# Rows for a gather pass: GpSimd's indirect gathers, and one tile in 64 by one-row transfers from SyncE

## The chip, the cores and the metric

The program runs on one core of a Trainium2 chip. The metric is the device time of one execution in microseconds; it is given as the median of several runs. The core has five engines that run side by side: TensorE (PE), VectorE (DVE), ScalarE (ACT), GpSimd (POOL) and SyncE (SP). SP and ACT issue direct DMAs, POOL issues indirect ones (a gather of rows by a list of row numbers).

## The reference, cut to what matters

A graph with 12,500 nodes of 128 features and 200,000 edges, sorted by destination. Four layers follow each other, each a sum over the edges of rows of a table with one row per node:

```
edge_index = jnp.stack([src, dst])
h = jnp.maximum(_layernorm(x, axis=-1), 0.0)
x = x + _L0_gnn_ref(h, edge_index, W1, b1, W2, b2)     # two graph convolutions: segment_sum(h[s] * norm, d)
h = jnp.maximum(_layernorm(x, axis=-1), 0.0)
x = x + _L1_gnn_ref(h, W, b, src, dst)                 # segment_sum(features[src], dst)
h = jnp.maximum(_layernorm(x, axis=-1), 0.0)
x = x + _L2_gnn_ref(h, edge_index, edge_weight, W, b)  # weighted segment_sum(x_lin[row] * norm, col)
h = jnp.maximum(_layernorm(x, axis=-1), 0.0)
x = x + _L3_gnn_ref(h, node_vec1, src, dst, ...)       # attention: exp, silu(bn(.)), segment_sum(msg, dst)
```

So the rows `table[src[e]]` are needed for all 200,000 edges, five times over: passes 0 to 2 (parts of bf16), pass 3 (weighted, f32), pass 4 (attention).

## The kernel before, in words

The edges stand in 1,563 tiles of 128 edges, eight tiles to a group (GT), 196 groups (TGROUPS). The nodes stand in 98 windows of 128. Before each pass the node table is written to HBM: `table16` (`table_parts`) for passes 0 to 2, 768 bytes a row in three parts of bf16, `table` for pass 3, 512 bytes a row in f32.

In a pass, four engines work in step through semaphores:
- POOL (`gather_tiles`, issue on L447) gathers one tile by one indirect DMA: partition e of the tile gets the table's row of edge e, by the numbers in `idx_tab`. The tiles go to a ring of eight groups (RGROUPS, 64 tiles) in SBUF. From group 8 on it waits at `s_free` until the group that held the place before is released.
- SP (`relay_rows`) waits at L456 until all tiles of a group have landed (`gathered`, one semaphore per group of the ring, its due count from `landed_count`), and hands the group over by one count of `s_landed`, two groups (LEAD) ahead of the release. For the release of group g it waits on `s_prod` for the number that the table RELEASE gives (read by `table_values`, L471, four at a time) and counts up `s_free` (L467). In the kernel before this is written out group by group.
- TensorE multiplies each tile with a one-hot matrix of its destinations and adds into PSUM, one bank per window (L604 in passes 0 to 2, L677 in pass 3), sixteen items to a half, in loops (`halves_in_loops`); it waits for `s_landed` and for open banks. It reads where each item goes by loads of 32 words (`plan_values`, L508).
- ScalarE or VectorE builds the one-hot matrices (L554 and L561, or L642) and the other one empties the banks (L583, L658).

`pass_in_parts` runs passes 0 to 2, `pass_with_weights` pass 3. Pass 4 has its own code, with the same gathers from `ptable`.

The setup (one block of the program) loads and reorders the index tables. On SP it starts with two loads of every 128th destination (L793, L796, into `last_i`, semaphore `s_last`); copies of the edge arrays follow (L803 to L809), and the load of `src` into `idx_tab` (L811 to L816). VectorE waits for `s_last` before L937 and computes from it the tile numbers (L947) with which POOL starts its first gathers (L764). `Steps` counts the serial steps of VectorE on `s_dve`; other engines wait for fixed counts of it.

## Time and profile before

| | us |
|---|---|
| Median of 3 runs | 11,316.48 |
| Lowest and highest | 11,309.37, 11,317.57 |
| The profiled execution | 11,348.41 |
| Its span, first to last instruction | 11,346.6 |
| Granted share of TensorE's clock over the span | 0.597 |

The profile's page gives busy time per engine, groups of instructions by line, and the idle time of the engine before them with the engine that ended it. "Issue" as a releaser means that the engine waited for nothing that the profile shows. Register work, semaphore instructions and the issue of DMAs are not busy time; SP does only these, so its busy time isn't listed, and its instructions are read from the timeline and from the view of one source line. PEq, SPq and the like are the sequencers of the engines.

### The profile page before, as it was taken

To read this page: it belongs to the slowest core of one execution; us is meant where nothing else is said; L and a number is where in the kernel's file an instruction comes from. 1 tells how busy PE (TensorE), PEld (TensorE's weight loads), DVE (VectorE), ACT (ScalarE), POOL (GpSimd) and SP (SyncE) were. 2 spreads that over 40 slices of the span, in tenths; PEclk is the share of its full clock that TensorE was granted. 3 is DMA by queue.
4 is the path that set the end of the run, shared out by engine and by line. 5 is a ranking of instruction groups with operands and counts; after the bars stand their busy time and mean duration, and the time that the engine had idled before them with its cause. 6 is when DMAs were issued, how large, how long until landed. Compare 5 with 4: busy or idle time off the path is not lost. (4 is left out here: it accounts for less than half of the span.)

```text
span 11346.6 us, 83949 instructions
## 1 busy us (share of the span) xinstructions
PE 4273.1 (38%) x19462; PEld 3000.1 (26%) x19463; DVE 3429.0 (30%) x7384; ACT 3213.0 (28%) x7261; POOL 8251.9 (73%) x8365
## 2 busy tenths in 40 slices
PE   1222222342222223223333433333354333334687
PEld 0111111121111112111111333333354333333576
DVE  4000001110001112000000422222235677777898
ACT  3333333343333334333333300000021111111465
POOL 5777777757777775777777677777766777777676
PEclk5555555665555555555555665655676555555799
DMA  4222222232222223222222212221214555555454
GB/s 104 78 79 79 79 79 79 74 87 79 79 79 79 79 79 100 78 79 79 78 78 78 62 52 52 52 52 53 53 46 137 156 159 164 164 164 168 149 168 134
DMA packets 676090, 1067.87 MB, mean 94 GB/s; under 512 B 150850, under 2 KB 518729, under 8 KB 648857
## 3 DMA queue, kind: packets, MB, share of 16 engines
q0 software_dynamic: 329072, 676.05, 22.8%
q10 hardware_dynamic: 247712, 225.10, 6.1%
q1 hardware_dynamic: 98985, 163.50, 4.4%
q14 instruction: 249, 2.04, 0.1%
q8 instruction: 72, 1.18, 0.0%
HBM read 904.63 MB, written 161.05 MB: 94 GB/s over the span
## 5 line engine op out<-in xcount | busy, mean ns | idle before, releaser
L447 POOL DMA_INDIRECT big<-table_parts,tile_cols x4689 | 4453.3, 950 | 1593.1 <-issue 1428.9
L604 PE MATMUL psum<-big 128*128 x4992 | 1724.3, 504 | 4129.3 <-SPq L456 4030.3
L604 PEld LDWEIGHTS psum<-big 128*128 128x128 bf16 x4992 | 663.9, 140 | 4928.4 <-issue 2683.2
L447 POOL DMA_INDIRECT big<-ptable,tile_cols x1563 | 1512.1, 967 | 498.7 <-issue 476.3
L447 POOL DMA_INDIRECT big<-table,tile_cols x1563 | 1485.9, 951 | 478.7 <-issue 476.2
L561 ACT ACTIVATE big<-big,ones 128x2048 bf16<-128x2048 bf16 x312 | 624.4, 2001 | 3707.5 <-PE psum L604 2469.5
L554 ACT ACTIVATE big<-iota_col,dl_tab 128x128 bf16<-128x128 f32 x4992 | 1490.6, 387 | 33.7 <-PEq L731 13.3
L1617 PE MATMUL psum<-acc,big 128*128 x3328 | 788.4, 420 | 1217.5 <-DVE big L1594 1205.1
L583 DVE TENSOR_REDUCE acc<-psum 128x128 f32<-128x384 f32 (+1 forms) x196 | 109.7, 560 | 3648.4 <-PE psum L608 1829.2
L677 PE MATMUL psum<-big 128*128 x3328 | 751.9, 418 | 1201.8 <-SPq L456 750.1
L1617 PEld LDWEIGHTS psum<-acc,big 128*128 128x128 f32 x3328 | 704.9, 317 | 1300.9 <-issue 1300.6
L677 PEld LDWEIGHTS psum<-big 128*128 128x128 f32 x3328 | 702.7, 322 | 1252.4 <-issue 633.9
L642 DVE TENSOR_SCALAR big<-iota_col,dl_tab,ew_tab 128x128 f32<-128x128 f32 x1664 | 438.4, 364 | 1516.8 <-PE psum L677 1510.0
L1571 DVE TENSOR_REDUCE wide<-big 128x128 f32<-128x2048 f32 x208 | 766.2, 3684 | 3.2 <-ACT big L1650 3.2
L1594 DVE SCALAR_TENSOR_TENSOR big<-big,sc,psum 128x130 f32<-128x130 f32 x1664 | 516.7, 344 | 567.6 <-SPq L456 332.7
L583 DVE TENSOR_REDUCE big<-psum 128x128 f32<-128x384 f32 x98 | 54.7, 558 | 1766.2 <-PE psum L604 1764.9
L658 ACT COPY acc<-psum 128x128 f32<-128x128 f32 x98 | 26.1, 267 | 1899.1 <-PE psum L677 1899.1
L1835 PE MATMUL psum<-big 128*128 128x129 f32 x3328 | 545.8, 298 | 37.2 <-POOL big L1756 35.0
L1755 POOL TENSOR_TENSOR big<-big,tile_cols 128x2048 f32<-128x2048 f32 x104 | 376.2, 3617 | 111.0 <-ACT big L1796 110.8
L1835 PEld LDWEIGHTS psum<-big 128*128 128x128 f32 x3328 | 427.3, 194 | 66.3 <-issue 51.4
L1650 ACT ACTIVATE big<-big 128x2048 f32<-128x2048 f32 x104 | 199.6, 1920 | 718.2 <-DVE wide L1575 713.8
L608 PE MATMUL psum<-big 128*128 x1664 | 349.2, 210 | 0.0
(300 smaller groups left out, 4274.1 us busy)
## 6 DMA issues: line engine op xcount, KB each, us to landing
big<-dl_rows ACTq DMA_DIRECT2D x104, 1024.0 KB
zrows<-big ACTq DMA_DIRECT2D x104, 1024.0 KB
big<-zrows SPq DMA_DIRECT2D x104, 1024.0 KB
big<-table_parts,tile_cols POOLq DMA_INDIRECT x4689, 2.6
table_parts<-big SPq DMA_DIRECT2D x42, 672.0 KB, 3.5
big<-table,tile_cols POOLq DMA_INDIRECT x1563, 2.5
big<-ptable,tile_cols POOLq DMA_INDIRECT x1563, 2.6
ptable<-big SPq DMA_DIRECT2D x14, 455.0 KB, 3.9
```

Source lines behind the costliest of these rows:

```text
L447: pool.indirect_dma_start(out=slots[:, t % (groups * GT), 0:width], out_offset=None, in_=tab, in_offset=bass.IndirectOffsetOnAxis(ap=idx_t ...
L554: last = nc.scalar.activation(apart_flat[:, u * P:(u + 1) * P], iota_col[:], ACT.Abs, bias=dl_tab[:, col:col + 1], scale=-1.0)
L561: nc.scalar.activation(half, apart_flat, ACT.Relu, bias=ones[:, 0:1], scale=-1.0).then_inc(s_onehot, 1)
L604: last = nc.tensor.matmul(held, m, rows_t, start=False, stop=False, skip_group_check=True)
L608: last = nc.tensor.matmul(held, m, weights, start=False, stop=False, skip_group_check=True)
L642: last = nc.vector.tensor_scalar(wide_onehot[:, q % 2 * HALF + u, :], iota_col[:], dl_tab[:, col:col + 1], ew_tab[:, col:col + 1], ALU.is_ ...
L677: last = nc.tensor.matmul(held, wide_onehot[:, a % 2 * HALF + u, :], rows_t, start=False, stop=False, skip_group_check=True)
L1571: nc.vector.tensor_reduce(part[:, k, :], rows_of, AX.X, ALU.add).then_inc(s_part, 1)
L1594: last = nc.vector.scalar_tensor_tensor(zbuf[:, h, u, 0:ACW], dyn(ring_flat, slots[u], ACW), in_win[:, h, u:u + 1], bank[n % Z_BANKS][:, 0 ...
L1617: last = nc.tensor.matmul(bank[u % Z_BANKS][:, 0:ACW], onehot_t[:, h, u * P:(u + 1) * P], dyn(acc_flat, at[u], ACW), start=True, stop=True)
L1755: nc.gpsimd.tensor_tensor(m[:, :, 0:F], m[:, :, 0:F], over_f(weights_of(q), HALF), ALU.mult)
L1835: nc.tensor.matmul(dyn(sums_at, at[u], SCW), onehot[:, q % 2 * HALF + u, :], msg[q % MSGS][:, u, 0:SCW], start=False, stop=False, skip_gro ...
```

## The change

In passes 0 to 3 (`no < PASSES - 1`), the last tile of every eighth group (`SIDE`: groups 8, 16, ... 184, 23 of them) is no longer gathered by POOL. SP fetches its 128 rows by 128 transfers of one row each from the table in HBM, at an address that it holds in a register, into the same place of the ring. It does so in a loop over turns of eight groups (`relay_with_side_rows`): after handing over a group and releasing another it issues 21 or 22 rows, in six steps of eight (SIDE_STEPS); ahead of the seventh hand-over it waits for all of them (`s_side`) and clears the semaphore. The row numbers are loaded 32 words at a time (SIDE_LOAD) from `side_of`, two tables (4 partitions of 23 x 32 words) that the setup loads from `src` by two more DMAs and VectorE multiplies by the bytes of a row, 768 and 512. The counts of the semaphores follow: `landed_count` leaves the tile out, `s_last` is due at 64 in place of 32, and the steps of VectorE have one more. Hand-overs before and behind the loop are written out by `relay_steps`. The tensor `rows` gets more partitions, not more columns. Pass 4 keeps `relay_rows`, which now calls `relay_steps`.

```diff
@@ -10,6 +10,8 @@
 READY_STEP = 4
 RGROUPS = 8
 LEAD = 2
+SIDE_FIRST, SIDE_EVERY, SIDE_STEPS = 8, 8, 6
+SIDE_LOAD = 32
 Z_RGROUPS = 4
 Z_LEAD = 2
 BLOCK = 8
@@ -75,6 +77,11 @@
     RSLOTS = RGROUPS * GT
     assert TGROUPS == -(-NT // GT) and 2 * SLOTS * ACW >= RSLOTS * F
     NTAB = NI + BODY
+    SIDE = list(range(SIDE_FIRST, TGROUPS - RGROUPS + LEAD + 1, SIDE_EVERY))
+    SIDE_SPAN = SIDE_EVERY * GT * P
+    SIDE_BASE = (SIDE_FIRST + 1) * GT * P - SIDE_SPAN
+    SIDE_TURNS = len(SIDE)
+    assert SIDE_FIRST == SIDE_EVERY == RGROUPS and RGROUPS - SIDE_STEPS == LEAD and SIDE_BASE + len(SIDE) * SIDE_SPAN <= E
     CHUNKS = NW // CW
     assert CHUNKS * CW == NW and NI % P == 0 and TILES >= TROWS >= NT
     IG = NI // P
@@ -178,10 +185,13 @@
         w_z = sb("w_z", [P, 2, SCW])
         b1c = sb("b1c", [P, HM])
         score_tab = ew_tab[:, 0:NI]
-        rows_all = sb("rows", [13, max(7 * SCW, NI // 2, PLAN_HALVES * PLAN_WORDS)])
+        SIDE_PARTS = P // SIDE_LOAD
+        rows_all = sb("rows", [64 + SIDE_PARTS, max(7 * SCW, NI // 2, PLAN_HALVES * PLAN_WORDS)])
         rows = rows_all[0:1, 0:7 * SCW].rearrange("o (a f) -> o a f", f=SCW)
 
 
+        assert SIDE_TURNS * SIDE_LOAD <= rows_all.shape[1]
+        side_of = [rows_all[32 * k:32 * k + SIDE_PARTS, 0:SIDE_TURNS * SIDE_LOAD].bitcast(i32) for k in (1, 2)]
         WIN, SLOT = (rows_all[k:k + 1, :].bitcast(i16) for k in range(1, 3))
         READY, RELEASE = (rows_all[k:k + 1, :].bitcast(u16) for k in range(3, 5))
         SUM_AT = rows_all[5:6, :].bitcast(i16)
@@ -427,13 +437,18 @@
         gathered = [sem(f"gathered{k}") for k in range(RGROUPS)]
         s_landed = [sem(f"rows_landed{no}") for no in range(PASSES)]
         s_free = sem("rows_free")
+        s_side = sem("side_rows")
 
         def tiles_of(g):
             return min(GT, NT - g * GT)
 
+        def has_side(no, g):
+
+            return no < PASSES - 1 and g in SIDE
+
         def landed_count(no, g):
 
-            return 16 * sum(tiles_of(k) for n in range(no + 1)
+            return 16 * sum(tiles_of(k) - has_side(n, k) for n in range(no + 1)
                             for k in range(g % RGROUPS, g + 1 if n == no else TGROUPS, RGROUPS))
 
         def gather_tiles(pool, no, tab, slots, groups, width):
@@ -442,29 +457,67 @@
             for g in range(TGROUPS):
                 if g >= groups:
                     pool.wait_ge(s_free, freed + g - groups + 1)
-                for k in range(tiles_of(g)):
+                for k in range(tiles_of(g) - has_side(no, g)):
                     t = g * GT + k
                     pool.indirect_dma_start(
                         out=slots[:, t % (groups * GT), 0:width], out_offset=None, in_=tab,
                         in_offset=bass.IndirectOffsetOnAxis(ap=idx_tab[:, t // P, t % P:t % P + 1], axis=0),
                     ).then_inc(gathered[g % RGROUPS], 16)
 
-        def relay_rows(sp, no, groups, lead, s_done, done0):
-
-            def landed(g):
-                sp.wait_ge(gathered[g % RGROUPS], landed_count(no, g))
-                sp.sem_inc(s_landed[no], 1)
-
-            for g in range(lead):
-                landed(g)
-            for g in range(TGROUPS):
+        def relay_steps(sp, no, steps, groups, lead, s_done, done0):
+
+            for g in steps:
                 if g + lead < TGROUPS:
-                    landed(g + lead)
-                if g + groups < TGROUPS:
+                    sp.wait_ge(gathered[(g + lead) % RGROUPS], landed_count(no, g + lead))
+                    sp.sem_inc(s_landed[no], 1)
+                if 0 <= g < TGROUPS - groups:
                     if g % 4 == 0:
                         releases = table_values(sp, RELEASE, g, 4, NI)
                     sp.wait_ge(s_done, releases[g % 4] + done0)
                     sp.sem_inc(s_free, 1)
+
+        def relay_rows(sp, no, groups, lead, s_done, done0):
+
+            relay_steps(sp, no, range(-lead, TGROUPS), groups, lead, s_done, done0)
+
+        def relay_with_side_rows(sp, no, tab, slots, width, kind, row_bytes):
+
+            flat, size = tab.rearrange("n f -> (n f)").unsqueeze(0), row_bytes // width
+            items0 = no * NI
+
+            def landed_in_turn(turn, g):
+                counts = [landed_count(no, n * SIDE_EVERY + g) for n in range(SIDE_TURNS)]
+                assert all(c == counts[0] + n * (counts[1] - counts[0]) for n, c in enumerate(counts))
+                return turn * (counts[1] - counts[0]) + counts[0]
+
+            def fetch(turn, j, numbers):
+                for e in range(j * P // SIDE_STEPS, (j + 1) * P // SIDE_STEPS):
+                    if e % SIDE_LOAD == 0:
+                        numbers.clear()
+                        words = [nc.alloc_registers(f"side{no}_{e + i}", engines=[SP]) for i in range(SIDE_LOAD)]
+                        c = e // SIDE_LOAD
+                        nc.regs_load(words, side_of[kind][c:c + 1, bass.ds(turn * SIDE_LOAD, SIDE_LOAD)])
+                        numbers.extend(nc.snap(word, engines=[SP], donate=True, min_val=0, max_val=(N - 1) * row_bytes,
+                                               guaranteed_mod_val=0, out_of_modulus=row_bytes) for word in words)
+                    at = numbers[e % SIDE_LOAD] // size
+                    sp.dma_start(slots[e:e + 1, GT - 1, 0:width], flat[:, bass.ds(at, width)]).then_inc(s_side, 16)
+
+            relay_steps(sp, no, range(-LEAD, 0), RGROUPS, LEAD, s_prod, items0)
+            with sp.Fori(0, SIDE_TURNS) as turn:
+                numbers = []
+                for j in range(SIDE_EVERY):
+                    if j == SIDE_STEPS:
+                        sp.wait_ge(s_side, 16 * P)
+                        sp.sem_clear(s_side)
+                    sp.wait_ge(gathered[(j + LEAD) % RGROUPS], landed_in_turn(turn, j + LEAD))
+                    sp.sem_inc(s_landed[no], 1)
+                    if j % 4 == 0:
+                        releases = table_values(sp, RELEASE, turn * SIDE_EVERY + j, 4, NI)
+                    sp.wait_ge(s_prod, releases[j % 4] + items0)
+                    sp.sem_inc(s_free, 1)
+                    if j < SIDE_STEPS:
+                        fetch(turn, j, numbers)
+            relay_steps(sp, no, range(SIDE_TURNS * SIDE_EVERY, TGROUPS), RGROUPS, LEAD, s_prod, items0)
 
         def table_values(eng, tab, start, n, largest):
 
@@ -544,7 +597,7 @@
 
                 @block.sync
                 def _(sp):
-                    relay_rows(sp, no, RGROUPS, LEAD, s_prod, items0)
+                    relay_with_side_rows(sp, no, table16, ring16, NPARTS * F, 0, 2 * NPARTS * F)
 
                 @block.scalar
                 def _(act):
@@ -630,7 +683,7 @@
 
                 @block.sync
                 def _(sp):
-                    relay_rows(sp, no, RGROUPS, LEAD, s_prod, items0)
+                    relay_with_side_rows(sp, no, table, ring32, F, 1, 4 * F)
 
                 @block.vector
                 def _(dve):
@@ -796,6 +849,9 @@
                     sp.dma_start(last_i[0:LASTS - many * P, many:many + 1], rest).then_inc(s_last, 16)
                 else:
                     sp.sem_inc(s_last, 16)
+                side_src = src[SIDE_BASE:SIDE_BASE + len(SIDE) * SIDE_SPAN].rearrange("(k s) -> k s", s=SIDE_SPAN)[:, SIDE_SPAN - P:]
+                for to in side_of:
+                    sp.dma_start(to.rearrange("c (k e) -> c k e", e=SIDE_LOAD), side_src.rearrange("k (c e) -> c k e", e=SIDE_LOAD)).then_inc(s_last, 16)
                 sp.wait_ge(s_pad, 4)
                 full = (NT - 1) * P
                 for rows_of, a, pad, s_copied in ((dst_rows, dst, pads.bitcast(i32)[:, P:2 * P], s_rows),
@@ -913,7 +969,7 @@
                     if 1 <= t <= CHUNKS:
                         ln.relu(act, t - 1, (t - 1) % 2)
 
-                act.wait_ge(s_dve, 15)
+                act.wait_ge(s_dve, 16)
                 nc.scalar.activation(deg_r, deg, ACT.Sqrt).then_inc(s_cnt, 1)
                 act.wait_ge(s_srck, -(-TB // 4))
                 for t in range(CHUNKS + 1):
@@ -932,8 +988,10 @@
                 nc.vector.memset(tile_cnt[:, NW:NW + 1], float(E // P))
                 dve.wait_ge(s_const, 1)
                 nc.vector.tensor_scalar(is_node[:], node_id[:, 0:NW], float(N), None, ALU.is_lt)
-                dve.wait_ge(s_last, 32)
-                step = Steps(dve, s_dve, 0, 3)
+                dve.wait_ge(s_last, 64)
+                nc.vector.tensor_scalar(side_of[0], side_of[0], 2 * NPARTS * F, None, ALU.mult)
+                step = Steps(dve, s_dve, 0, 4)
+                step(nc.vector.tensor_scalar(side_of[1], side_of[1], 4 * F, None, ALU.mult))
                 nc.vector.tensor_scalar(last_wi, last_i, P.bit_length() - 1, None, ALU.arith_shift_right)
                 step(nc.vector.tensor_scalar(last_pi, last_i, P - 1, None, ALU.bitwise_and))
                 nc.vector.tensor_copy(last_w, last_wi)
@@ -949,7 +1007,7 @@
                 step.end()
 
                 dve.wait_ge(s_starts, 1)
-                step = Steps(dve, s_dve, 3, 10)
+                step = Steps(dve, s_dve, 4, 10)
                 step(nc.vector.tensor_tensor(bound[:, 0:NW], bank[5][:, 0:NW], wplus1[:, 0:NW], ALU.add))
 
                 step(nc.vector.tensor_tensor(le, bound[:, 0:NW].unsqueeze(1).to_broadcast([P, IG, NW]),
@@ -1034,7 +1092,7 @@
                     if 2 <= t < IG + 2:
                         keep_dl(t - 2)
 
-                step = Steps(dve, s_dve, 3 + 10, 3)
+                step = Steps(dve, s_dve, 4 + 10, 3)
                 dve.wait_ge(s_degrees, 1)
                 step(nc.vector.tensor_tensor(deg, bank[4][:, 0:NW], row_ptr[:, 0:NW], ALU.subtract))
                 nc.vector.tensor_scalar(no_edges[:], deg, 0.0, None, ALU.is_equal)
@@ -1061,7 +1119,7 @@
                     nc.tensor.matmul(bank[4][:, 0:NW], below[:, b, :], same[:, b, :], start=b == 0, stop=False)
                     last = nc.tensor.matmul(bank[4][:, 0:NW], ones[:], before[:, b, :], start=False, stop=b == IG - 1)
                 last.then_inc(s_counted, 1)
-                pe.wait_ge(s_dve, 3)
+                pe.wait_ge(s_dve, 4)
                 nc.tensor.matmul(bank[5][:, 0:NW], first, tile_cnt[:, 1:NW + 1], start=True, stop=True).then_inc(s_starts, 1)
                 pe.wait_ge(s_weights, 16 * 17)
                 nc.tensor.transpose(bank[6][:, 0:F], wload[:, 0, :], ident[:])
```

## Rows read from the trace of the kernel before

**Rows 1.** The page: busy times, the gathers' groups, a landing time.
```profile
PE 4273.1 (38%) x19462; PEld 3000.1 (26%) x19463; DVE 3429.0 (30%) x7384; ACT 3213.0 (28%) x7261; POOL 8251.9 (73%) x8365
...
L447 POOL DMA_INDIRECT big<-table_parts,tile_cols x4689 | 4453.3, 950 | 1593.1 <-issue 1428.9
L447 POOL DMA_INDIRECT big<-ptable,tile_cols x1563 | 1512.1, 967 | 498.7 <-issue 476.3
L447 POOL DMA_INDIRECT big<-table,tile_cols x1563 | 1485.9, 951 | 478.7 <-issue 476.2
...
big<-table_parts,tile_cols POOLq DMA_INDIRECT x4689, 2.6
```

**Rows 2.** Busy time by stretch: passes 0, 3 and 4 (last: DMA share, GB/s).
```profile
core 0: us, PE busy (x) PEld busy (x) DVE busy (x) ACT busy (x) POOL busy (x), PEclk, DMA share, GB/s
268.00:2227.00 1959.00, 567.92 (x1668) 217.25 (x1667) 126.74 (x388) 703.94 (x1765) 1482.81 (x1563) 0.55 0.29 79
...
6459.00:8420.00 1961.00, 759.58 (x3317) 702.40 (x3316) 437.54 (x1662) 51.47 (x194) 1484.79 (x1562) 0.59 0.20 52
8570.00:10558.00 1988.00, 782.78 (x3304) 699.76 (x3304) 1419.97 (x2679) 230.30 (x306) 1511.71 (x1563) 0.57 0.55 161
```

**Rows 3.** Waits of POOL, passes 0 to 3: us in total, times, longest.
```profile
POOL big L447 <- issue: 1905.2, 6248, 0.3
```

**Rows 4.** Waits of SP in pass 0: us in total, times, longest.
```profile
SPq L456 <- DMA big<-table_parts,tile_cols: 1902.0, 196, 12.1
```

**Rows 5.** Timeline of TensorE in pass 0: start, us, what, [idle before, releaser].
```profile
359.31 2.72 PE L604 MATMUL psum<-big 128*128 x8 [7.25 <-SPq L456]
```

**Rows 6.** Timeline of SP: DMA instructions of the setup (start us, us).
```profile
0.89 0.47 SPq L793 DMA_DIRECT2D big<-in_dst  x1
1.41 0.73 SPq L796 DMA_DIRECT2D big<-in_dst  x1
...
3.52 0.44 SPq L806 DMA_DIRECT2D dst_rows<-big  x1
...
8.34 0.25 SPq L816 DMA_DIRECT2D tile_cols<-in_src  x1
8.64 2.75 SPq L819 DMA_DIRECT2D wide<-in_L_gnn_b  x3
```

**Rows 7.** Sequencer work by source line: duration in ns, min/median/max; first, last start.
```profile
L722 SPq DMA_DIRECT2D table_parts<-big x42: 372/372/406, 218.4 to 4367.9; - x42
L722 SPq FUSED_REGOPS  x12: 64/64/76, 2278.2 to 2347.4; - x12
L722 SPq MOVE table_parts<-big x12: 29/29/29, 2278.3 to 2347.5; - x12
...
L421 SPq FUSED_REGOPS  x14: 80/80/94, 6363.0 to 6454.5; - x14
L421 SPq ALU_OP  x14: 32/33/37, 6363.2 to 6454.6; - x14
L421 SPq MOVE table<-acc x14: 34/34/34, 6363.2 to 6454.6; - x14
L421 SPq DMA_DIRECT2D table<-acc x14: 383/384/418, 6363.3 to 6454.7; - x14
...
L419 SPq COMPARE_BRANCH  x14: 44/45/50, 6363.8 to 6455.2; - x14
...
L508 PEldq TENSOR_LOAD <-rows x416: 2128/2159/2199, 271.5 to 8412.3; - x139
```

**Rows 8.** Timeline of the setup: a store by SP beside a gather by POOL.
```profile
111.31 0.32 SPq L837 DMA_DIRECT2D dl_rows<-big  x1
...
111.54 0.95 POOL L764 DMA_INDIRECT big<-dst_rows,big  x1 [0.30 <-issue]
```

**Rows 9.** Timelines of VectorE and POOL, the start of the setup.
```profile
15.91 1.49 DVE L955 TENSOR_TENSOR big<-big 128x1274 f32<-128x1274 f32 x1
...
15.71 1.15 POOL L764 DMA_INDIRECT big<-dst_rows,big  x1 [10.46 <-DVE big L947]
```

## The prediction

> **What bounds the kernel now.** I read the page first. GpSimd (POOL) is busy 73% of the span, twice any other compute engine; the indirect gathers on L447 make up 7,451 us of that [rows 1]. The table by stages then shows the passes that the change touches: the first of the four lasts 1,959 us, the fourth 1,961, with 1,563 gathers each [rows 2]. That is 1.254 us a gather, though one takes 0.95 us. The waits of POOL say what the rest is: 6,248 gaps of 0.3 us put down to "issue", that is to no other engine, and inside the passes no wait on SyncE (SP), which frees the ring [rows 3]. So POOL runs gather after gather at a fixed pace and nothing holds it back. The others wait for it: SP stands 1,902 of a pass's 1,959 us at L456 for gathered tiles [rows 4], and TensorE works 2.7 us in every 10 [rows 5]. A gather less is therefore 1.254 us less, as long as SP, which hands over every group, keeps pace.
>
> **What is removed.** SIDE has 23 groups (8, 16, ... 184), one tile each, in passes 0 to 3: 92 gathers. 92 x 1.254 = 115.4 us. It is all on the path, since POOL never waits inside these passes. What is late next? After 56 gathers for 7 whole groups and 7 for the eighth, POOL needs 63 x 1.254 = 79.0 us for a turn of eight groups (80.3 before).
>
> **What is added: SP's turn.** Each turn SP issues 128 one-row transfers, so all hangs on what one costs SP, in issue and not in bytes. The trace has no run of one-row loads with a register's address in HBM, so I bound it.
> - The nearest row: one row of 0.2 KB from HBM into SBUF (L816) took 0.25 us on SP, and the next instruction started 0.05 us later [rows 6]. That is 0.30 us, the lower end.
> - The register address. The looped store at L722 shows, for each transfer whose address comes from the loop, a FUSED_REGOPS (64 ns) and a MOVE (29 ns); L421 shows FUSED_REGOPS 80, ALU_OP 33, MOVE 34 [rows 7]. Here the address is a byte count that is loaded ready; the code divides it by the size of an element and the addressing multiplies it back, so I expect the arithmetic to go and the MOVE to stay: 0.034 and one more gap of 0.045. I take 0.25 + 0.034 + 2 x 0.045 = 0.377 us a row.
> - The upper end with L816's issue and L421's full chain: 0.253 + 0.147 + 4 x 0.045 = 0.58 us. If the issue too cost what a looped transfer of 128 partitions costs (0.384, L421), it would be 0.71 us. I take the low value because the row it is nearest to in shape is L816, and the register's address hardly lengthens the DMA instruction itself: L722 has 372 at both kinds, minimum and median.
>
> Other work of SP in a turn: four loads of 32 words, by PE's at L508 2.16 us each (with 0.06 of address work 8.9 us) [rows 7]; the eight hand-overs and two release loads, which are in the trace: 1,959 - 1,902 = 57 us for 196 groups, so 2.3 us for eight; register arithmetic for waits and the branch, by L419's 32 to 45 ns each, some 1.3 us [rows 7]. Sum 12.5 us. So a turn is
> - taken: 128 x 0.377 + 12.5 = 60.8 us;
> - lower end (0.30): 50.9 us;
> - upper end (0.58): 86.7 us; extreme (0.71): 103.5 us.
>
> Against 79.0 us of POOL the taken value leaves 18 us. The break-even follows from the ring. SP's first turn starts when three groups are in (30 us), and after its last turn POOL has about five groups left (50 us), so a pass that SP bounds takes 80 + 23 T. POOL alone would take 1,540 x 1.254 = 1,931. These meet at T = 80.5, a row of 0.53 us. Below that the saving is whole, above it each 0.01 us of a row costs 128 x 23 x 4 x 0.01 = 118 us in all: a cliff.
>
> **Moved and queued behind.** The 21 or 22 rows of a step stand in front of SP's next hand-over. At 0.377 us they are 8.0 to 8.3 us, 8.9 to 10.6 with a load, against 10.0 us between groups, so a hand-over is late by a few us and steps 6 and 7, without rows, catch up. Behind it wait TensorE, idle 7.3 us of each group [rows 5], and `s_free`; POOL needs the release of group g only at g+8, some five groups after it is due. Cost nothing; cover gone only when SP is behind by 50 us, which is the cliff above. The wait on `s_side` before group 8n+8 is handed over comes one group after the last row was issued; landings take 2.6 us in the median [rows 1]; at worst TensorE gets that group some 3 us late.
>
> **Do SP's transfers slow POOL's gathers?** In the setup SP issued the 64 KB store L837 at 111.31 beside a gather that began at 111.54: gather 0.95, gap 0.30, as ever [rows 8]. I take nothing. Upper bound: in the last gather pass, where ACT moves 1 MB pieces beside it, 1,563 gathers took 1,988 us, 1.272 each [rows 2]. The bytes that move in a pass stay what they are, at a DMA share of 0.29.
>
> **Setup.** Two more transfers stand on SP behind L796, and VectorE waits for both ahead of L937, plus two integer multiplications of 736 columns in 4 partitions. L793 and L796 took 0.47 and 0.73 us [rows 6]; two like them, landing later, hold VectorE 1.3 to 3 us; the multiplications, by L955 (1,274 columns, 1.49 us), 0.9 us each [rows 9]. POOL's first gather at 15.71 waits for this chain (L947) [rows 9]. I take +4 us, between 2 and 8; a gain is excluded, nothing there gets shorter.
>
> **Sum.** The profiled execution took 11,348.4 us (span 11,346.6 and 1.8 around it); 11,348.4 - 115.4 + 4 = 11,237.0. The median of the shown runs, 11,316.5, is 31.9 below the profiled one; with the same distance: **11,205 us**, 1.0% less.
>
> **A rule that speaks against it.** What the rows show: a DMA instruction of SP takes 0.25 us for one row [rows 6] and 0.37 to 0.38 for 7 x 128 rows in the steady loops [rows 7]. The Trainium skill, page "DMA: Bandwidth & Descriptors", in its comparison under "Why a DMA increments its semaphore by 16 and not by 1", gives 512 sequencer cycles for each such instruction on generations before the newest, whatever its size; at the 1.2 GHz that "Advanced Engine Details and Errata", section Clock Domains, gives for SP this is an estimate of 0.43 us. By that rule SP's row would be 0.43 + 0.034 + 0.09 = 0.55 us, past the cliff. The trace disagrees, with every steady row of SP below 0.43, so I give it little. As a mechanism of this kernel it is rival 2.
>
> Of instruction fetch the page "Runtime: NRT & Kernel Launch", section "Instruction fetch mechanics", says that a taken branch to a page no longer held stalls the engine. No row here shows SP in so long a loop; a stall of 1 to 3 us a turn would be inside the 18 us left.
>
> **Rivals.**
> 1. SP becomes the bound by the full address chain: 0.58 us a row. Place: the sequencer of SP, in the 23 turns of each pass. A pass takes 80 + 23 x 86.7 = 2,074 us, 115 more than now; four: 11,348.4 + 460 + 4 = 11,812, as a median 11,780 us. It decides from 0.53 us a row. For: the looped transfers do carry that arithmetic [rows 7], and the setup's back-to-back small transfers went up to 0.7 us [rows 6]. Against: the address is loaded ready. With 0.71 us it would be about 13,300.
> 2. A row at 0.55 us (a DMA instruction of 0.42 to 0.44, as L806 had for one row of 0.2 KB the other way, to HBM [rows 6]): T = 83, pass 80 + 1,909 = 1,989; +30 x 4 + 4: 11,472, as a median 11,440 us.
> 3. SP's stream slows every gather to the pace of the last pass: 1,540 x 4 x 0.019 = +117 us takes back the whole 115: about 11,320 us, no change. Against it stands [rows 8].
> 4. The change does less than it says: SP late by so much in a turn that POOL loses part of each, half the gain left: 11,262 us.
>
> **Chances.** Forecast 0.70; rival 1 0.15; rival 2 0.06; rival 3 0.05; rival 4 0.04. Own range of the forecast 11,192 to 11,235 (setup 2 to 8 us, gathers at 1.25 to 1.27 in part). The range that should hold 8 in 10: 11,190 to 11,560; its top is a row of 0.56 us, between rivals 2 and 1; the 0.58 and 0.71 ends are what is left out with about 0.13. A measurement of this kernel tells 0.2%, 23 us, from no change. Faster: 0.70 + 0.04 - 0.01 = 0.73; within: 0.06; slower: 0.15 + 0.06 = 0.21.
>
> **What would show it.** POOL's gaps in passes 0 to 3 still "issue" alone, 6,160 gathers of those kinds, passes of 1,931 us: forecast right. A wait of POOL on SP's release (L467's successor) says the cliff. The source view of the new transfer gives its price: 0.25 with a MOVE alone is my step, 0.43 rival 2, a FUSED_REGOPS each rival 1. SP's waits for gathered tiles should keep 18 of 79 us a turn, some 400 us a pass. Gathers at 1.27 us without POOL waiting would be rival 3. POOL's first gather later than 24 us would put the setup cost wrong. The prediction fails if a row costs SP more than 0.53 us.

## The result, and the profile after

| | before, us | after, us |
|---|---|---|
| Median of 4 runs | 11,317.02 (11,309.37 to 11,317.73) | **11,202.47** (11,193.88 to 11,204.21) |
| The profiled execution | 11,348.41 | 11,202.09 |

The ratio is 0.990, with a 95% interval of 0.9884 to 0.9915: the change makes the kernel 1.0% faster here, 114.6 us by the medians. Later runs qualify that. Where the kernel before itself takes some 12,900 us, the changed kernel is 8% slower than it. The experiments below tell of both.

The page of the changed kernel: busy times, the gathers' groups, two lines of the DMA issues (they answer to [rows 1]).

```profile
span 11200.3 us, 109030 instructions
PE 4264.5 (38%) x19462; PEld 2992.0 (27%) x19463; DVE 3432.3 (31%) x7386; ACT 3212.2 (29%) x7261; POOL 8132.6 (73%) x8273
...
L462 POOL DMA_INDIRECT big<-table_parts,tile_cols x4620 | 4371.5, 946 | 1570.2 <-issue 1407.3
L462 POOL DMA_INDIRECT big<-ptable,tile_cols x1563 | 1501.4, 961 | 497.3 <-issue 476.0
L462 POOL DMA_INDIRECT big<-table,tile_cols x1540 | 1460.3, 948 | 471.7 <-issue 469.2
...
big<-table_parts SPq DMA_DIRECT2D x8832, 0.8 KB
...
big<-table SPq DMA_DIRECT2D x2944, 0.5 KB
```

The 92 gathers are gone (4,620 + 1,540 in place of 4,689 + 1,563), and 8,832 + 2,944 = 11,776 = 92 x 128 transfers of SP have come. POOL's waits in passes 0 to 3 (us in total, times, longest) answer to [rows 3]; there is still no wait on SP among those of the gathers:

```profile
POOL big L462 <- issue: 1876.5, 6156, 0.3
```

The view of the transfer's line, and of the load of its 32 row numbers, on SP (duration in ns min/median/max; first and last start):

```profile
L503 SPq MOVE big<-table_parts x8832: 29/29/38, 302.4 to 6128.4; - x197
L503 SPq DMA_DIRECT2D big<-table_parts x8832: 219/224/352, 302.5 to 6128.5; - x197
...
L499 SPq FUSED_REGOPS  x368: 46/52/61, 300.4 to 8168.2; - x184
L499 SPq TENSOR_LOAD <-rows x368: 1865/2029/2196, 300.5 to 8168.3; - x184
```

A row costs one MOVE and one transfer: no arithmetic per row. From one row's start to the next the median is 0.318 us, worked out from all of them. The waits of SP in passes 0 to 3 (they answer to [rows 4]):

```profile
SPq L513 <- DMA big<-table_parts,tile_cols: 1520.8, 344, 10.0
SPq L513 <- DMA big<-table,tile_cols: 530.0, 115, 9.9
...
SPq L511 <- DMA big<-table_parts: 95.6, 69, 1.6
```

The last line and one like it for pass 3 (29.1 us, 23 times) are the waits for the side rows, 1.4 us each on average. All four together are 2,175.5 us over 92 turns, 23.7 us a turn. A turn lasts 78.8 us, so SP works 55.1 of it.

The table by stretches (first to last gather of passes 0, 3 and 4; columns as in [rows 2]):

```profile
268.00:2192.00 1924.00, 570.60 (x1666) 218.28 (x1665) 126.62 (x388) 703.95 (x1765) 1455.17 (x1539) 0.55 0.30 80
6355.00:8283.00 1928.00, 755.54 (x3315) 697.46 (x3314) 440.23 (x1662) 51.38 (x194) 1459.09 (x1539) 0.60 0.20 53
8432.00:10408.00 1976.00, 777.82 (x3304) 695.56 (x3304) 1414.87 (x2678) 230.31 (x306) 1500.30 (x1562) 0.58 0.56 162
```

Passes 0 and 3 are 35 and 33 us shorter than [rows 2] has them. Pass 4, which the change leaves alone, is 12 us shorter too. That tells the reader to look at the pace of the gathers itself. The gathers of pass 1, of the kernel before and then of the changed one:

```profile
L447 POOL DMA_INDIRECT big<-table_parts,tile_cols x1563: 942/949/1004, 2352.0 to 4310.3; - x196
```
```profile
L462 POOL DMA_INDIRECT big<-table_parts,tile_cols x1540: 942/946/1082, 2316.3 to 4240.9; - x193
```

(4,310.3 - 2,352.0) / 1,562 = 1.2537 us before, (4,240.9 - 2,316.3) / 1,539 = 1.2506 after. The 3 ns a gather make some 24 us over 7,723 gathers. Neither the change nor its rows make them. Each trace of this document has one of two paces, and it can be told from the gathers' median duration: 0.949 us here, in e0, and with the change in e7; 0.946 us in the changed kernel's profile above and, without a row fetched, in e12. The profiled execution of the kernel before took 11,348 us where its other runs took 11,309 to 11,318, and the slower pace accounts for 24 of these 32 us. The two profiled executions therefore differ by 146 us and the medians by 114.6. The medians agree with the removed gathers alone: 92 x 1.251 = 115.1.

### The profile page after: what moved, and what is told of

It reads as the page before. It is cut to its first block and busy times, and to the rows that moved or that the text cites. A ratio compares the mean times of both kernels' runs of the same rounds, so it can differ in the third digit from the quotient of the medians.

```text
span 11200.3 us, 109030 instructions
## 1 busy us (share of the span) xinstructions
PE 4264.5 (38%) x19462; PEld 2992.0 (27%) x19463; DVE 3432.3 (31%) x7386; ACT 3212.2 (29%) x7261; POOL 8132.6 (73%) x8273
## 5 line engine op out<-in xcount | busy, mean ns | idle before, releaser
L462 POOL DMA_INDIRECT big<-table_parts,tile_cols x4620 | 4371.5, 946 | 1570.2 <-issue 1407.3
L462 POOL DMA_INDIRECT big<-table,tile_cols x1540 | 1460.3, 948 | 471.7 <-issue 469.2
```

What stands on the lines that cost most here:

```text
L462: pool.indirect_dma_start(out=slots[:, t % (groups * GT), 0:width], out_offset=None, in_=tab, in_offset=bass.IndirectOffsetOnAxis(ap=idx_t ...
```

## The experiments

There are four groups of runs; each group ran on one chip and has its own runs of the kernel before. The kernel before did not take the same time in each, which turned out to be the main finding:

| Group | Chip | Kernel before, median us | Runs |
|---|---|---|---|
| 1 | 4 | 12,883.82 | e0, e1, e2, e4 |
| 2 | 2 | 12,950.10 | e6, e7, e8, e9 |
| 3 | 6 | 12,935.96 | e10, e11 |
| 4 | 4 | 11,316.46 | e12, e13 |

Groups 1 and 4 are on the same chip number, 70 minutes apart. So the chip number doesn't decide it; the condition was there in one group and not in the other. I call groups 1 to 3 the slow groups. TensorE's granted clock doesn't explain them: 0.593 in e0, against 0.597.

In e1, e10, e12 and e13 the 92 tiles are fetched by nobody; these kernels compute with stale rows there.

**e0: the kernel before, once more.** No edit.

> The kernel before, unchanged, profiled once more. In the first profile of it a gather of POOL came every 1.254 us (most common interval), in the profile of the changed kernel every 1.251 us, in the setup too, which the change leaves alone there; and the profile of before was 32 us above the median of its runs while that of after is not above its own. Theory A (a slower execution was profiled, nothing of the kernel's): the new profile shows 1.250 to 1.251 us a gather, pass 0 of 1,953 to 1,955 us for 1,563 gathers, and a time of 11,310 to 11,325. Theory B (the change itself makes POOL's gathers 3 ns quicker, since SP now moves rows): 1.254 again and about 11,345.

Measured: 12,904.82 us, one run. It is the same program as in [rows 1] (83,949 instructions in both pages). The gathers, the waits of POOL in passes 0 to 3 (up to 9,480 us here), and those of SP in pass 0:

```profile
L447 POOL DMA_INDIRECT big<-table_parts,tile_cols x4689: 943/949/1442, 277.3 to 7109.3; - x196
L447 POOL DMA_INDIRECT big<-table,tile_cols x1563: 942/947/1077, 7254.1 to 9471.8; - x196
L447 POOL DMA_INDIRECT big<-ptable,tile_cols x1563: 942/947/1271, 9632.0 to 12100.0; - x196
```
```profile
POOL big L447 <- issue: 1859.4, 6029, 2.6
POOL big L447 <- SPq L467: 1040.8, 219, 11.2
```
```profile
SPq L467 <- remote: 1797.1, 118, 23.8
SPq L467 <- PE psum L604: 60.9, 22, 6.9
SPq L456 <- DMA big<-table_parts,tile_cols: 12.1, 1, 12.1
```

Set against [rows 3] and [rows 4] this is another kernel: SP stands 12 us for gathered tiles in place of 1,902 and waits for the matmuls' count instead, and POOL waits 219 times for a release. The counts come late: of SP's 171 waits at L467 of over 1 us in pass 0, 104 ended more than 5 us after the last matmul that counts had ended, up to 21 us. The gather as such is as it was (0.949 us in the median). The cover on which the prediction builds, that SP waits for POOL, isn't there in the slow groups even without the change. Nor is the condition one of passes 0 to 3 alone. Of the 1,556 us by which e0's span is longer, they have 1,005; the gathers of pass 4, which the change leaves alone, take 2,468 us in place of 1,988 [rows 2], 480 more. The two expectations spoke of the gathers' pace: it is again that of the slower profile, but in a time that neither of them had, and e7 and e12 below tell that it isn't the change that sets it.

**e1: no side rows at all.** Everything of the change but the transfers, the loads of the row numbers and the side wait.

```diff
-                    if j == SIDE_STEPS:
-                        sp.wait_ge(s_side, 16 * P)
-                        sp.sem_clear(s_side)
-                    if j < SIDE_STEPS:
-                        fetch(turn, j, numbers)
```

> SP's 128 one-row transfers per turn, their register loads and the wait for them are left out; POOL still leaves the 92 tiles out, so those tiles hold old rows and the output is not the reference's. Theory A (SP's work is hidden whole, and its transfers cost POOL nothing): the time stays that of the changed kernel, 11,195 to 11,208 us, passes of 1,925 us, POOL 1.251 us a gather. Rival 3 (SP's stream slows the gathers): faster than the changed kernel by up to 1,540 x 4 x 0.003 = 18 us and more, so below 11,185. Rival 4 (SP late, part of the gain lost): below 11,185 as well, with a wait of POOL gone that the changed kernel would have had to show.

Measured: 12,768.02 us, ratio 0.991 (0.9893 to 0.9926). Fewer gathers are worth 0.9% in a slow group too. What makes the changed kernel lose there (below) is in the lines that this run leaves out.

**e2, e9, e11: the loads of row numbers five times over.** Meant as a dial on SP's turn.

```diff
-                        nc.regs_load(words, side_of[kind][c:c + 1, bass.ds(turn * SIDE_LOAD, SIDE_LOAD)])
+                        for _ in range(5):
+                            nc.regs_load(words, side_of[kind][c:c + 1, bass.ds(turn * SIDE_LOAD, SIDE_LOAD)])
```

> Each load of 32 row numbers by SP is done five times in place of once: 16 more loads of 2.10 us in a turn of eight groups, nothing else. In the changed kernel SP works 55.1 us of a turn of 78.8 (the waits for gathers and rows make up 23.7); now 55.1 + 33.6 = 88.7 us. Theory A (the cliff, a pass bounded by SP takes 80 + 23 T): passes 0 to 3 of 80 + 2,040 = 2,120 us against 1,925, so 11,202 + 4 x 195 = 11,980 us, and POOL is seen to wait for SP's release. Rival (SP has no part in the bound, its lateness is absorbed by the ring of eight groups): 11,200 us, as before the edit.

> 16 more loads of 2.10 us on SP in each turn of eight groups, once more. T = 88.7 us. Theory A (cliff, a pass takes 80 + 23 T): passes 0 to 3 of 2,120 us, 11,980 us in all, POOL waits on SP's release. Rival (the ring takes it all up): as the changed kernel. If this chip too has late counts, slower than 11,980 by the same per cent as on the other.

> 16 more loads of 2.10 us on SP in each turn of eight groups (T = 88.7 us), a third time, for a chip of the first kind. There, theory A (cliff, a pass takes 80 + 23 T): passes 0 to 3 of 2,120 us, 11,980 us in all, POOL waits on SP's release; rival (the ring takes it up): 11,200. On a chip like 2 and 4: 14,000 again.

Measured: 13,996.72, 14,028.55 and 13,972.38 us; ratios 1.087 (1.0853 to 1.0894), 1.082 (1.0783 to 1.0864), 1.080 (1.0783 to 1.0823). The edit did nothing. The view of the load in e2 has as many as the changed kernel, and its page has the same 109,030 instructions: the repeated loads, whose results are overwritten unread, were dropped when the kernel was built.

```profile
L500 SPq TENSOR_LOAD <-rows x368: 5/1982/2085, 315.2 to 10485.7; - x184
```

So these three say nothing of the dial. They are three more measurements of the changed kernel, and the first sign that it loses 8% in the slow groups. By the time alone they would pass for the cliff of theory A; the number of loads in the view shows that it isn't that.

**e7: the changed kernel, once more.** No edit.

> The changed kernel as it is, as the reference for the kernels beside it. On the chip of the runs above, the kernel before took 12,884 us and not 11,317, its passes 2,200 us and not 1,959, because POOL there waited for SP's release, and SP for TensorE's count of products, which came up to 20 us and more behind the last matmul; on the chip of the first profiles it comes 0.5 us behind. Theory A (the saving is 92 gathers where POOL alone bounds the passes): beside a kernel before of about 11,317, 11,200 us, ratio 0.990. If the kernel before is at about 12,880 here, the hand-over is part of the bound and SP's rows have less cover: then slower than the kernel without rows (e1, 0.991), by up to some per cent.

Measured: 14,017.34 us, ratio 1.082 (1.0784 to 1.0857). Waits of POOL in passes 0 to 3 (up to 10,536 us here), the gathers of the first three, and the view of the transfer's line:

```profile
POOL big L462 <- SPq L517: 2205.5, 380, 15.6
POOL big L462 <- issue: 1783.2, 5732, 1.7
```
```profile
L462 POOL DMA_INDIRECT big<-table_parts,tile_cols x4620: 943/949/1369, 277.5 to 7933.7; - x193
```
```profile
L503 SPq MOVE big<-table_parts x8832: 1/29/1401, 313.8 to 7875.1; - x197
L503 SPq DMA_DIRECT2D big<-table_parts x8832: 1/224/1450, 314.5 to 7875.1; - x197
```

The medians are unchanged, but look at the ends: 1 ns and 1.4 us. The timeline of SP over 16 us, of the changed kernel as first measured and then of e7 (start, us, what, how many), shows what that is:

```profile
331.35 12.51 SPq L503 DMA_DIRECT2D big<-table_parts  x32
```
```profile
328.50 16.79 SPq L503 DMA_DIRECT2D big<-table_parts  x7
```

In such stretches a MOVE and a transfer alike come at steps of 1.4 us. In turns 7 to 22 of pass 0 the 128 rows take 80.6 us of a turn (0.63 each) against 47.4 (0.37 each), the time to the instruction behind each row counted, waits among it; and a turn is 101.2 us long, of which SP waits some 3. SP bounds the pass. By the prediction's formula a pass then takes 80 + 23 x 98 = 2,334 us, or 2,408 with SP's waits counted in; 2,472 were measured. So the cliff is real and, by SP's records, it is at SP, but the row crossed it for a reason that the prediction didn't have.

**e4, e8: the full address chain.** The tables keep row numbers, and SP multiplies each one; the multiplication on VectorE goes.

```diff
-                        numbers.extend(nc.snap(word, engines=[SP], donate=True, min_val=0, max_val=(N - 1) * row_bytes,
-                                               guaranteed_mod_val=0, out_of_modulus=row_bytes) for word in words)
-                    at = numbers[e % SIDE_LOAD] // size
+                        numbers.extend(nc.snap(word, engines=[SP], donate=True, min_val=0, max_val=N - 1) for word in words)
+                    at = numbers[e % SIDE_LOAD] * width
```

> The setup no longer multiplies the row numbers (no integer multiplications by VectorE); SP computes each address from the row's number. Theory A (price by the source lines: MOVE 29 ns and DMA 224 ns in the changed kernel, 0.318 us a row with gaps): each row gets a FUSED_REGOPS of 50 to 80 ns and a gap more, 0.42 us a row, so a turn of SP is 55.1 + 128 x 0.10 = 68 us, still below 78.8; the time stays at 11,195 to 11,208 us. Rival 1 of the prediction (the full chain passes the cliff: 0.58 us a row, T = 88): 11,950 us.

> The address of each row worked out by SP from the row's number, once more, since the chip of the first try had the hand-over in the bound. There a row came every 0.409 us in place of 0.319 (median). Theory A (cliff at T = 80.5 us a turn, constants of the first chip): T = 55.1 + 128 x 0.09 = 66.6 us, time as the changed kernel, within 10 us. Theory B (the rows cost from the first nanosecond on, since they delay hand-overs that TensorE waits for): slower than the changed kernel by tens of us or more.

Measured: 14,765.90 us, 1.147 (1.1446 to 1.1485); and 14,635.32 us, 1.131 (1.1273 to 1.1353). The source view of e8 shows the one instruction more per row, which rival 1 was built on:

```profile
L502 SPq FUSED_REGOPS  x11776: 1/37/1396, 310.5 to 11014.2; - x200
```

It is one FUSED_REGOPS of 37 ns and not a FUSED_REGOPS and an ALU_OP: the row's median pitch goes from 0.318 to 0.409 us. By these medians rival 1's price of 0.58 doesn't appear even with the chain. In a slow group the instruction costs 618 us (14,635 - 14,017), or 52 ns a row.

**e6: three tiles in sixteen groups.** SP fetches 33 tiles a pass in place of 23; the core of the edit:

```diff
-SIDE_FIRST, SIDE_EVERY, SIDE_STEPS = 8, 8, 6
+TURN, SIDE_AT = 16, (8, 12, 16)
+SIDE_STEPS_OF = ((0, 1, 3, 4), (5, 6, 8, 9), (10, 11, 12, 13))
```

> Three tiles in sixteen groups by SP in place of two: 33 in a pass in place of 23, the loop over 11 turns of 16 groups, rows 32 at a time in twelve of the sixteen steps. POOL has 1,530 gathers a pass: 1,530 x 1.2505 = 1,913 us. SP's turn: 384 rows x 0.319 + 12 loads x 2.16 + 4 release loads x 1.08 + 16 hand-overs, together 160 us, against 156 of POOL. Theory A (ring absorbs what SP is behind, 4 us x 11 turns): passes of 1,913 to 1,920 us, 11,155 to 11,185 us. Rival (SP already at its limit, a late hand-over costs): slower than the changed kernel, from 11,220 us.

Measured: 15,418.73 us, ratio 1.190 (1.1865 to 1.1942). A slow group can't answer what this asked, the gain where SP has time left. It does show that the loss grows with the rows: 1,249 us over e1 for 92 tiles (e7), 2,651 for 132.

**e10: each row's MOVE and transfer replaced by two counts of a semaphore.** As many instructions on SP, nothing moved, no loads.

```diff
-                    sp.dma_start(slots[e:e + 1, GT - 1, 0:width], flat[:, bass.ds(at, width)]).then_inc(s_side, 16)
+                    sp.sem_inc(s_side, 1)
+                    sp.sem_inc(s_side, 1)
...
-                        sp.wait_ge(s_side, 16 * P)
+                        sp.wait_ge(s_side, 2 * P)
```

> Each row's MOVE and transfer on SP is replaced by two one-count semaphore instructions on s_side; the row loads go too. No row is fetched (the 92 tiles hold old rows, the output is not the reference's); POOL leaves the 92 tiles out. SP has as many instructions as in the changed kernel, no transfers, and less time in them. On chips 2 and 4 the changed kernel or its variants took 13,980 to 14,770 us against 12,884 and 12,950 before, the one without rows 12,768; there SP's records of rows lie on a grid of 0.7 us for stretches, with some instructions of 1 to 4 ns. Theory R (on those chips a cost per recorded instruction, some 50 ns each: 1,249 us for 23,552 more in e7 than e1, 618 us for 11,776 more in e8 than e7): if this runs on such a chip, 13,900 to 14,100. Theory D (the transfers themselves hurt there, by the DMA engines or the memory): about 12,770. On a chip of the first kind both say 11,195 to 11,208, since SP's turn is 25 us of 78.8.

Measured: 13,259.28 us, ratio 1.026 (1.0236 to 1.0284), between the two expectations: 491 us above e1, 758 below e7 (other groups' kernels before differ by 0.5%, some 65 us). The view of one of the two counts:

```profile
L503 SPq EVENT_SEMAPHORE  x11040: 1/17/1408, 314.7 to 9709.9; - x198
```

The 1.4 us are there without a transfer. In turns 7 to 22 of pass 0 the counts recorded at the two lines, 239 a turn, take 70 us, 0.29 each. A count that nothing holds is followed by SP's next instruction after some 0.07 us (e13 below). So the stretching needs no transfer; it holds for counts of SP too. It is seen on SP alone: of its register, branch and semaphore instructions 130 of 2,963 took over 0.3 us in e0, 1,915 of 15,895 in e7 and 4,903 of 27,301 in e10, against 1 in each of the two traces of the result, while POOL, ScalarE and VectorE have 0 to 4 of theirs in all of these. About 40% of the loss comes back with the instructions alone; for the rest the transfers and the loads are needed, or that SP is past the cliff and no longer only near it.

**e12, e13: SP's time by the clock, without rows.** On e1's base SP reads words of a table, waits for a value long reached and counts; 5 times (e12) or 7 times (e13) in each of the six steps.

```diff
+                    if j < SIDE_STEPS:
+                        for n in (5, 6, 7, 8, 9):      # e13: (5, 6, 7, 8, 9, 10, 11)
+                            again = table_values(sp, RELEASE, turn * SIDE_EVERY + j, n, NI)
+                            sp.wait_ge(s_prod, again[0] + items0)
+                            sp.sem_inc(s_side, 1)
```

> SyncE's loop over turns without the one-row transfers, without the rows' addresses, without the side wait (POOL leaves the 92 tiles out, they stay stale). In their place SyncE makes 5 reads of 5 to 9 u16 words per group in six groups of each turn, each followed by a wait that has long been met and one count: 30 reads, estimated at 56 us a turn from the 0.85 to 1.04 us that a read of four words takes, so some 61 us of work per turn of SyncE with 90 instructions where the change has over 260. The theory 'SyncE's time alone makes the loss on the slower chips' expects the loss of the changed kernel, a ratio of 1.08, where the kernel before takes some 12,900 us. The theory 'it is what the many short instructions and the transfers put on the recording path and the queue, not SyncE's time' expects the ratio of the kernel without rows, 0.991 (range 0.985 to 1.00). On a chip where the kernel before takes 11,317 us both expect 0.99, since the turn of SyncE (61 us) lies under POOL's 79.

> As the run with 60 us, but 7 reads of 5 to 11 words per group: some 92 us of SyncE's work per turn (87 for the reads, 5 for the rest), above the turn of POOL. The prediction's own slope: a pass bounded by SyncE takes 80 + 23 T. With T = 92 that is 2,196 us where 1,925 was measured, 4 x 271 = 1,084 us more than the changed kernel, so near 12,290 us and a ratio of 1.086 on a chip where the kernel before takes 11,317. On a chip where it takes 12,900 (passes of some 2,200 us there) a bound by SyncE's time gives passes near 2,200 to 2,300 and a ratio of 1.00 to 1.04; the rival by which SyncE's lateness adds to what the slower chip already loses expects 1.15 or more.

Measured, in the group where the kernel before takes 11,316: e12 11,198.56 us, ratio 0.990 (0.9881 to 0.9914); e13 11,579.65 us, 1.023 (1.0216 to 1.025). The reads cost less than I estimated: from 0.85 us for four words to 2.25 us for eleven, 0.2 us a word. Waits of SP in e12 for gathered tiles at the looped hand-over:

```profile
SPq L510 <- DMA big<-table_parts,tile_cols: 1842.7, 538, 10.0
SPq L510 <- DMA big<-table,tile_cols: 593.8, 184, 10.0
```

2,436.5 us over 92 turns are 26.5 of 78.8 us, so SP works 52 us a turn, near the changed kernel's 55. And the time is that of the changed kernel to 4 us, though not a row is fetched. That settles rival 3 for this condition: 11,776 transfers beside the gathers cost them nothing measurable. The gathers' pace is the same too:

```profile
L462 POOL DMA_INDIRECT big<-table_parts,tile_cols x4620: 942/946/1449, 266.7 to 6231.3; - x193
```

e13 doesn't reach the 92 us of work a turn that I aimed at. A turn less SP's waits is 77 us of work in pass 0 and 81 in passes 1 to 3. The 4 us between them are additions: the loop adds the pass's first item (`items0`) to each number that it waits for, which in pass 0 is an addition of 0 and isn't in the program. From pass 1 on a turn has 52 ALU_OPs more, 42 of them at this line, 0.033 us each and a gap; the first is at 2,364 us, in pass 1.

```profile
L518 SPq ALU_OP  x2898: 32/33/43, 2364.2 to 8610.1; - x194
```

Waits of POOL in passes 0 to 3 (up to 8,670 us here), of SP for matmuls in pass 0 and then in pass 1, and the gathers of passes 0 and 2:

```profile
POOL big L462 <- SPq L514: 415.4, 159, 4.5
```
```profile
SPq L514 <- PE psum L657: 83.3, 40, 5.6
```
```profile
SPq L514 <- PE psum L657: 78.6, 39, 5.3
```
```profile
L462 POOL DMA_INDIRECT big<-table_parts,tile_cols x1540: 940/946/1280, 267.1 to 2207.0; - x193
...
L462 POOL DMA_INDIRECT big<-table_parts,tile_cols x1540: 940/946/1418, 4421.6 to 6490.4; - x193
```

Worked out from the starts and ends of all of SP's records, over 22 turns of each pass:

| Pass | SP's work, us a turn | its wait for matmuls | the turn | 80 + 23 x the turn, us | gathers of the pass | changed kernel |
|---|---|---|---|---|---|---|
| 0 | 77.3 | 3.6 | 80.9 | 1,940 | 1,940 | 1,925 |
| 1 | 81.3 | 3.4 | 84.7 | 2,027 | 2,028 | 1,925 |
| 2 | 81.2 | 5.3 | 86.5 | 2,070 | 2,069 | 1,926 |
| 3 | 81.2 | 4.5 | 85.7 | 2,050 | 2,051 | 1,929 |

The run as a whole is 377 us slower than the changed kernel. The prediction's formula holds to 1 us if T is the whole turn, which says that the ends of a pass still take 80 us. It fails if T is SP's work alone, as the prediction had it: 77.3 would cost nothing and 81.2 some 20 us a pass, about 65 in all. The rest is SP's wait at the release, 3.4 to 5.3 us a turn in every pass, for matmuls which themselves wait for SP's late hand-overs. SP's time and TensorE's then lie one behind the other in part, instead of beside each other. That this is what joins them is read from the waits; no run varies it.

## Why the prediction was right, and where it wasn't

- **The bound and the gain.** Right. POOL runs free, 92 gathers less at 1.25 us. The forecast, 11,205, is 3 us from the median. That the result was measured in the condition of the kernel before's first runs, and not in the one of groups 1 to 3, is luck: the prediction had no term for it.
- **The price of a row.** Right in kind, and 0.06 us too high in size: MOVE and transfer with no arithmetic, 0.029 and 0.224 us at a pitch of 0.318, where I took 0.377. The gaps were counted at 0.045 each and come to 0.065 for both. The instruction was 0.224 where one row of the setup took 0.253 [rows 6].
- **SP's turn.** 55.1 us where I had 60.8: the rows 41 for 48, the four loads 8.5 for 8.9. The rest of the turn, hand-overs, releases and branch, is 5.9 for 3.6. 24 us stay free. Of the stall of 1 to 3 us that the prediction allowed for behind the loop's branch there is no sign: SP's next instruction starts 0.23 us after the branch has ended.
- **The side wait.** 1.4 us each, hidden: as taken.
- **The setup.** I took +4 us. POOL's first gather starts at 16.83 where it was 15.71 [rows 9], a delay of 1.1, and pass 0 begins at 267.6 in both kernels, so nothing is left of it. VectorE's two multiplications took 0.53 us each, not 0.9.

```profile
5.39 0.53 DVE L992 TENSOR_SCALAR rows<-rows 4x736 int32<-4x736 int32 x1
...
16.83 1.15 POOL L817 DMA_INDIRECT big<-dst_rows,big  x1 [11.62 <-DVE big L1005]
```

- **The sum.** 11,237 in terms of the profiled execution against 11,202 is 35 us off. It is right as a median because I took the profiled execution's distance of 32 us as given; 24 of the 32 are gathers at 1.2537 in place of 1.2506 us.
- **Rival 2 and the rule behind it.** The Trainium skill, page "DMA: Bandwidth & Descriptors", section "Why a DMA increments its semaphore by 16 and not by 1", gives 512 sequencer cycles for each such instruction. The trace disagrees: 0.224 to 0.225 us in the median for 11,776 of them, half of the 0.43 that I estimated from it.
- **Rivals 1, 3 and 4.** Rival 1 had the wrong price: there is no arithmetic per row, and even with it (e4, e8) a row is 0.409 us. Rival 3 is false here, by e12. Rival 4 would have shown a wait of POOL on SP in passes 0 to 3, and there is none.
- **The cliff.** The mechanism is right and its point too far out. The prediction sets SP's work alone against POOL's turn, and has cover gone only when SP is 50 us behind. In e13 a pass is 15 us longer with 77 us of work and 103 to 142 us longer with 81, since SP's wait for matmuls comes on top. Where between 55 and 77 us it begins wasn't measured.
- **What wasn't in it at all.** The prediction holds SP's price of a row to be a property of the instruction. In three of four groups it isn't: there SP's instructions take up to 1.4 us each in stretches, a turn 101 us, and the changed kernel is 8% slower than the kernel before (e7, and e2, e9, e11). The forecast is right for the condition in which the kernel before takes 11,317 us and wrong for the other.

**What stays open** is the cause of the slow condition, and why counts on `s_prod` arrive late in it. One fact points at the recording: the trace of e0 holds 33,757 records of semaphore updates where that of the kernel before, the same program, holds 145,257; nearly all that are missing are of DMA landings (24,580 for 133,946). So it is in all ten traces of the slow groups, 33,757 to 64,696 records, and in none of the other four, 145,257 to 167,272. The other two fit it: the 1.4-us grid in the records of SP, and the growth of the loss with SP's instruction count. None of these shows that records hold an engine up and not just come late or get lost. By the Trainium skill, page "NOTIFIC — the notification-queue block", section "7.1 Overflow: three behaviours, one of which stalls the engine", a full ring drops records or, under one of its settings, stalls the producer, and the block's own pipeline always pushes back; no run here shows which setting holds. Another rival, that something else on the machine took time from HBM or the DMA engines, isn't tested either; against it stands that gathers which nothing holds up keep their 0.949 us and their gaps of 0.3 in e0. e12 was meant to tell SP's time from SP's instructions under the slow condition, and met the other one. A run of e12 beside a slow kernel before would do it. No complete version that beats both kernels came out: e12 equals the changed kernel in its group, e1 beats both kernels in its own (12,768 us), and both leave the 92 tiles out.

## What to carry to other kernels

Price work for an idle sequencer by the instruction, from a row of the same engine and shape, and add it up over the period in which the engine must hand something over: 128 rows at 0.32 us in 79 us fit, and 92 gathers at 1.25 us were gained whole. Keep more than the arithmetic margin: where the helper's lateness delays the work for whose end it then waits, the loss starts before its time equals the bound's period. And measure the kernel before beside every variant: the same change was worth 1% or cost 8% by a condition that the kernel before's own time gives away.

## What the runs showed of the hardware that I had not expected

- One and the same kernel took 11,316 and 12,884 us on chip number 4, 70 minutes apart, with a spread of 0.3% within each group and a granted clock of 0.60 and 0.59.
- A MOVE, a transfer or a count of SP took up to 1.4 us in the slow groups (e7, e10), in stretches of tens of us; otherwise, in the median, 0.029, 0.224 and 0.017.
- Back-to-back gathers have one of two paces, by the trace: medians of 0.949 us and 1.254 from one to the next, or 0.946 and 1.251. The changed kernel has the first in e7 and the second in the result, so the program doesn't decide it.
- A load into SP's registers costs by the word and by its kind: 32 words of int32 2.03 us, 63 ns each; 4 to 11 words of u16 0.85 to 2.25 us, 0.2 us each. The Trainium skill, page "Runtime: NRT & Kernel Launch", section "Instruction fetch mechanics", gives about 200 ns a register; that agrees for u16 and is three times too much for int32.
